# Causal masking of transposed scores on GpSimd instead of TensorE, with the last units and the stores of later query parts reordered

## What is computed

```python
q = q * cos + _rotate_half(q) * sin
k = k * cos + _rotate_half(k) * sin
qg = q.reshape(b, HKV, G, t, DH)                       # HKV 8, G 4, t 1024, DH 16
scores = jnp.einsum('bhgtd,bhkd->bhgtk', qg, k) / math.sqrt(DH)
scores = jnp.where(causal, scores, jnp.finfo(jnp.float32).min)
attn = jax.nn.softmax(scores, axis=-1)
ctx = jnp.einsum('bhgtk,bhkd->bhgtd', attn, v)
```

## Time and profile before

| | |
|---|---|
| median of 3 runs | 854.83 us (853.3 to 856.59) |
| the profiled execution | 854.79 us, span of its instructions 853.0 us |
| mean granted PE clock | 0.944 of full |
| PE busy | 751.9 us (88%) |
| DVE, ACT, POOL busy | 477.2, 314.7, 265.9 us |
| exponentials of the heads | from 91.4 us to 380.4 us |

### The profile page before, as it was taken

How to read it: one execution, slowest core, us unless ns; L and a number is a source line. 1 busy time by engine, 2 the same in 40 slices (tenths; PEclk the granted TensorE clock), 3 DMA queues, 4 the chain that set the end, 5 groups by cost and what they waited for, 6 DMA issues and landing times.

```text
span 853.0 us, 10154 instructions
## 1 busy us (share of the span) xinstructions
PE 751.9 (88%) x3710; PEld 444.2 (52%) x3710; DVE 477.2 (56%) x720; ACT 314.7 (37%) x528; POOL 265.9 (31%) x219
## 2 busy tenths in 40 slices
PE   5797983999999999879889999797778899997998
PEld 2343331333333333217658888543346688885886
DVE  3768761667776767306845637793687433336310
ACT  4211352566665656761315510244212322332100
POOL 0318547431312303151236513232223122222500
PEclk9997896999999999999989999998779899998999
DMA  9360623061321410212003300110320011111111
GB/s 323 129 122 2 146 65 83 1 146 44 68 84 27 110 64 1 91 38 62 0 27 112 97 1 1 52 41 1 48 63 29 25 50 49 49 39 36 61 62 38
DMA packets 24111, 53.00 MB, mean 62 GB/s; under 512 B 4252, under 2 KB 8100, under 8 KB 23044
## 3 DMA queue, kind: packets, MB, share of 16 engines
q1 hardware_dynamic: 24068, 52.44, 22.1%
HBM read 45.63 MB, written 6.60 MB: 61 GB/s over the span
## 4 chain that ended last, share of the span: by engine, by line
PE 67%; DVE 11%; issue 8%; POOL 8%; ACT 3%; DMA 2%; SPq 1%; ACTq 0%; POOLq 0%; DVEq 0%
PE ps L833 65%; DVE mxp L1688 2%; ACT pr L1374 2%; DVE xnb L1565 1%; DMA rq<-in_mask 1%; POOL wsum L2100 1%; PE ps L850 1%; PE ps L982 1%; POOL qacc L2070 1%; POOL qsw L2069 1%; POOL qacc L2073 1%; POOL qparts L2004 1%; DVE st L1543 1%; DVE arena L1572 1%; DVE dg L1912 1%
## 5 line engine op out<-in xcount | busy, mean ns | idle before, releaser
L833 PE MATMUL ps<-arena 128*128 128x512 f32 (+1 forms) x1416 | 333.6, 397 | 13.0 <-ACT full L1499 5.4
L833 PEld LDWEIGHTS ps<-arena 128*128 128x128 f32 (+1 forms) x1416 | 266.0, 189 | 74.7 <-DVE arena L1575 11.8
L1688 DVE TENSOR_REDUCE mxp<-ps 128x2 f32<-128x1024 f32 (+3 forms) x160 | 173.4, 1115 | 85.6 <-PE ps L833 69.2
L1374 ACT ACTIVATE pr<-ps 128x512 f32<-128x512 f32 x288 | 161.6, 596 | 118.8 <-PE ps L833 117.0
L833 PE MATMUL ps<-Qst,Kst 99*128 99x512 bf16 x288 | 106.1, 391 | 7.1 <-ACT pr L1374 4.2
L833 PE MATMUL ps<-Kst,Qst 96*128 96x512 bf16 (+3 forms) x384 | 102.6, 339 | 6.5 <-DVE mxp L1688 4.8
L833 PE MATMUL ps<-pr,vr 128*32 128x512 f32 x576 | 79.4, 624 | 0.7 <-ACT pr L1374 0.7
L833 PE MATMUL ps<-maskb,identb 128*128 128x128 bf16 (+1 forms) x320 | 75.3, 258 | 0.0
L833 PEld LDWEIGHTS ps<-Kst,Qst 96*128 96x128 bf16 x384 | 36.4, 100 | 73.1 <-DVE mxp L1688 27.5
L833 PEld LDWEIGHTS ps<-Qst,Kst 99*128 99x128 bf16 x288 | 27.3, 98 | 77.0 <-ACT pr L1374 58.4
L2191 POOL TENSOR_TENSOR arena<-raw,arena 128x1024 fp32r<-128x1024 f32 x11 | 26.6, 2418 | 85.8 <-ACT arena L1440 85.8
(11 more groups left out here) (190 smaller groups left out, 809.8 us busy)
## 6 DMA issues: line engine op xcount, KB each, us to landing
wmr<-in_wmr SPq DMA_DIRECT2D x8, 1280.0 KB, 6.4
raw<-in_w SPq DMA_DIRECT2D x16, 512.0 KB, 3.3
Qst<-q_parts SPq DMA_DIRECT2D x42, 128.0 KB
q_parts<-qparts SPq DMA_DIRECT2D x3, 768.0 KB, 8.5
x<-in_x SPq DMA_DIRECT2D x8, 256.0 KB, 5.9
wm<-in_wm SPq DMA_DIRECT2D x4, 512.0 KB, 7.1
raw<-in_up SPq DMA_DIRECT2D x8, 256.0 KB, 2.6
raw<-in_down SPq DMA_DIRECT2D x8, 256.0 KB, 2.7
```

What stands on the lines that cost most here:

```text
L833: return nc.tensor.matmul(outp, lhs, rhs, start=start, stop=stop, skip_group_check=True)
L1374: A(pr[:, k % PRING, :], ps[:, 4 + k % 2, :], ACT.Exp, scale=float(DH) ** -0.5).then_inc(exp_done, 1)
L1688: V.tensor_reduce(mxp[:, kh, g0:g0 + heads, i].rearrange("p (b e) -> p b e", e=per), units, AXX, ALU.max)\
```

## The change

It does six things.

- Chunk 1 of the later queries is stored ahead of `head_dmas(0)`, and chunk h+2 after the loads for head h+2 (h = 0, 1), so chunks 2 and 3 are stored ahead of `head_dmas(1)` and `head_dmas(2)`.
- DVE's wait for chunk 3 moves from the start of body 1 to `ctx_norm(0)`.
- For heads 1 to 7 the mask product of `t_unit` is left out. After the exponential GpSimd multiplies the four diagonal blocks, read as int32, by 0 or 1 (`cap`, made once by DVE). PE waits for `masked` before each `pv_round` whose round has a diagonal.
- Diagonal units come early: rounds 0 to 4 hold 1, 2, 2, 2 and 1 of them, rounds 5 to 8 none.
- `pv_round(n, r)` comes after unit 4r+7, for r up to 7, where it was 4r+5.
- "max" comes two units later (unit 26 in a steady body), and `weigh(n+1)` is cut into pieces, one per round from round 1, behind that round's masks.

```diff
@@ body_steps
-        out.append((max(step, 3) if what == "ctx" else step, what, d, s))
+        out.append((max(step, 3) if what == "ctx" else step + 2 * (what == "max"), what, d, s))
@@ transposed_units
-            units.append((r, p) if r <= p else (r - p - 1, NT - 1 - p))
+            if r <= p:
+                units.append((r, p))
+            else:
+                i = NT - 1 - p
+                units.append((i, i) if r == p + 1 else (r - p - 2, i))
...
+DIAG = [[k for k in range(4 * r, 4 * r + 4) if TUNITS[k][0] == TUNITS[k][1]] for r in range(ROUNDS)]
+DIAGS_TO = [sum(len(DIAG[q]) for q in range(r + 1)) for r in range(ROUNDS)]
+POOL_MASKED = 1
+def masks_by_gpsimd(n, r):
+    return NT * (n - POOL_MASKED) + DIAGS_TO[r]
...
+        cap = at("cap", [P, P], I32, HT_B + 28 * 1024)
@@ sync
+            def store_queries(c):
+                sp.wait_ge(part_q, c)
+                sp.dma_start(qscr[c, :, :, :].rearrange("q p t -> p q t"), qparts[:, :, :]).then_inc(q_out, 16)
+            store_queries(1)
             for h in range(NKV):
                 head_dmas(h)
-                if h < 3:
-                    sp.wait_ge(part_q, h + 1)
-                    sp.dma_start(qscr[h + 1, :, :, :].rearrange("q p t -> p q t"), qparts[:, :, :]).then_inc(q_out, 16)
                 if h < NKV - 2:
...
                     load_queries(h + 2, every, st_in[h + 2])
+                if h < 2:
+                    store_queries(h + 2)
@@ tensor, t_unit
-                last = mm(o, Kst[...], Qst[...], True, i > j)
-                if i == j:
+                by_pe = i == j and n < POOL_MASKED
+                last = mm(o, Kst[...], Qst[...], True, not by_pe)
+                if by_pe:
                     last = mm(o, identb[:, :], maskb[:, 1, :].unsqueeze(1).to_broadcast([P, G, P]), False, True)
@@ tensor, pv_round
                 pe.wait_ge(exp_done, n * NTU + 4 * r + 4)
+                if n >= POOL_MASKED and DIAG[r]:
+                    pe.wait_ge(masked, masks_by_gpsimd(n, r))
@@ tensor, head_body
-                    if k % 4 == 1:
-                        if k > 4:
-                            pv_round(n, k // 4 - 1)
-                        elif n:
-                            pv_round(n - 1, ROUNDS - 1)
+                    if k % 4 == 3 and k > 4:
+                        pv_round(n, k // 4 - 1)
+                    if k == 1 and n:
+                        pv_round(n - 1, ROUNDS - 1)
@@ vector
             V.tensor_copy(maskb[:, :, :].rearrange("p a b -> p (a b)"), rq[0][:, 0:2 * P]).then_inc(k_ones, 1)
+            V.tensor_scalar(cap[:, :], rq[0][:, P:2 * P], 0.0, None, ALU.is_ge).then_inc(cap_ready, 1)
...
+            dve.wait_ge(cap_ready, 1)
@@ vector, ctx_norm
+                if n == 0:
+                    dve.wait_ge(part_q, 3)
@@ vector, bodies
-                if n == 1:
-                    dve.wait_ge(part_q, 3)
@@ gpsimd
+            def mask_round(n, r):
+                for k in DIAG[r]:
+                    pool.wait_ge(exp_done, n * NTU + k + 1)
+                    v = pr[:, k % PRING, :].rearrange("p (g t) -> p g t", g=G).bitcast(I32)
+                    nc.gpsimd.tensor_tensor(v, v, cap[:, :].unsqueeze(1).to_broadcast([P, G, P]), ALU.mult).then_inc(masked, 1)
+            def head_pool(n):
+                head_v(n)
+                work = weighing(n + 1) if n < NKV - 1 else iter(())
+                for r in range(ROUNDS):
+                    mask_round(n, r)
+                    if r > 0:
+                        next(work, None)
+                for _ in work:
+                    pass
...
-            head_v(1)
-            weigh(2)
+            pool.wait_ge(cap_ready, 1)
+            head_pool(1)
...
             for n in range(2, NKV):
-                head_v(n)
-                if n < NKV - 1:
-                    weigh(n + 1)
+                head_pool(n)
```

More of the change, by code:

```diff
@@ L21 @@
 F32R = mybir.dt.float32r
+I32 = mybir.dt.int32
 BF16 = mybir.dt.bfloat16
@@ L378 @@
 for i in range(NT):
-    assert [j for j, k in TUNITS if k == i] == list(range(i + 1))
+    assert sorted(j for j, k in TUNITS if k == i) == list(range(i + 1))
+FIRST_J = [next(j for j, k in TUNITS if k == i) for i in range(NT)]
+LAST_J = [[j for j, k in TUNITS if k == i][-1] for i in range(NT)]
+DIAG = [[k for k in range(4 * r, 4 * r + 4) if TUNITS[k][0] == TUNITS[k][1]] for r in range(ROUNDS)]
+DIAGS_TO = [sum(len(DIAG[q]) for q in range(r + 1)) for r in range(ROUNDS)]
+assert DIAGS_TO[-1] == NT
+POOL_MASKED = 1
+def masks_by_gpsimd(n, r):
+    return NT * (n - POOL_MASKED) + DIAGS_TO[r]
 def adaln_two_blocks(nc, a, out):
@@ L560, in adaln_two_blocks @@
         sw_done = sem("later_queries_swapped")
+        cap_ready, masked = sem("cap_ready"), sem("diagonal_masked")
         kst_ones = sem("key_rows_of_ones_ready")
@@ L955, in t_unit @@
                 o = ps[:, 4 + k % 2, :].rearrange("p (g t) -> p g t", g=G)
-                last = mm(o, Kst[:, n % 3, j * P:(j + 1) * P], Qst[:, n % 3, :, i * P:(i + 1) * P], True, i > j)
-                if i == j:
+                by_pe = i == j and n < POOL_MASKED
+                last = mm(o, Kst[:, n % 3, j * P:(j + 1) * P], Qst[:, n % 3, :, i * P:(i + 1) * P], True, not by_pe)
+                if by_pe:
                     last = mm(o, identb[:, :], maskb[:, 1, :].unsqueeze(1).to_broadcast([P, G, P]), False, True)
@@ L971, in pv_round @@
                     q = 32 * strip(i)
-                    last = mm(ps[q:q + 32, 6 + i // 4, :], vr[:, j, :], pr[:, k % PRING, :], j == 0, j == i)
+                    last = mm(ps[q:q + 32, 6 + i // 4, :], vr[:, j, :], pr[:, k % PRING, :], j == FIRST_J[i],
+                              j == LAST_J[i])
                 last.then_inc(pv_done, 1)
@@ L2082, in head_v, with weighing @@
                 nc.gpsimd.tensor_copy(vr[:, :, 0:DH], vtok[:, :, n * DH:(n + 1) * DH]).then_inc(vr_ready, 1)
-            def weigh(h):
+            def weighing(h):
                 pool.wait_ge(wmr_in, 16 * h + 16)
@@ L2102, in weigh @@
                                 link(ins)
+                            yield
                 ins.then_inc(wsum_ready, 1)
+                yield
+            def weigh(h):
+                for _ in weighing(h):
+                    pass
[12 more added lines that the diff above has]
+                for _ in work:
+                    pass
             rope_queries(1)
```

## The result

The changed kernel takes 841.79 us (median of 4 runs, 840.46 to 843.66) where the kernel before takes 855.71 (853.3 to 856.6) beside it: a ratio of 0.9843 [0.9811, 0.9875]. The forecast was 828, the range 815 to 850. The sign and the range hold; the gain is 13.9 us in place of 26.8, about half. In the profiled executions the span falls from 853.0 to 838.6 us, by 14.4.

A forecast was written before the change was run, and what follows sets the result against it. PE was taken as the bound in the heads, with room on DVE, ACT and POOL. The sum: 854.8 - 16.3 - 9.1 - 8.0 + 1.5 + 4.0 + 0.3 + 1.0 = 828.2 us, range 815 to 850.

The forecast's parts named there:

- The stores: Early chunk stores bring chunk 3 forward and remove head 1's whole excess: 16.3 us gained, bounds 13.9 and 16.3.
- The mask products on PE: Mask products leave PE in heads 1 to 7: 9.1 us gained, bounds 5 and 12.3.
- "max" two units later: PE's hole before the turn of the maxima, waiting for nm, is covered: 8.0 us gained, bounds 4 and 11.2.
- mod late next: nothing: After the later "max", DVE's copy of "mod" has 2 us of other PE work ahead, so costs nothing.
- The small costs: DVE making cap in the prologue, 0.3 us, and maxima(1) beside chunk 3, 1.0 us, bounds 0 and 2.
- The split of the output weights: Pushed back by head 7's masks, done by 385 before the projection at 388.59: no cost, 3 us of cover.
- POOL's charges: Two costs of PE waiting for POOL: 1.5 us for masks over all heads, 4.0 us for weigh(3) in head 2.
- weigh(3) late in head 2: Head 3's eight-piece weigh ends late, PE stands before "mod" in head 2: 4.0 us cost, bounds 2 and 6.
- The waits for masks: POOL's 17.3 us before round 4 fit an 18.75 us window; short PE waits cost 1.5 us, bounds 0 and 6.
- The slow integer product: Rival: a GpSimd mask takes 2.56 us, GpSimd becomes the bound, kernel slower at 884.7 us; chance 0.14.
- The partly slow product: Rival: a GpSimd mask takes 1.75 us, adding 14 us of waits, 841 us in all; chance 0.14.
- Chunk 3: Rival: early stores don't bring chunk 3 forward, head 1's hole stays at 14 to 16 us, 844.5 us; chance 0.04.

The follow-up runs named there:

- e1: To the kernel before, only the early stores of the query chunks and DVE's wait moved to ctx_norm(0): 840.73 us, ratio 0.9847.
- e2: The changed kernel with the masks of all heads back on PE as products, GpSimd doing only weigh: 828.75 us, ratio 0.9698.
- e4: The changed kernel with weigh(n+2) done whole behind head n's masks, weigh(2) before head 1, its weights loaded earlier: 821.95 us, ratio 0.9628.
- e8: e1 plus "max" and pv_round both two units later, diagonals where they were, masks on PE: 831.73 us, ratio 0.9694.
- e6: The changed kernel with each GpSimd mask product done twice, the second waiting for the first: 909.34 us (2 runs), ratio 1.062.
- e3: The changed kernel with weighing pausing after its first product too, so the first piece is one product: 833.93 us, ratio 0.9769.

## Why the prediction was right or wrong

**The stores** (16.3): right for head 1, 16.34 by e1; by the medians e1 brings 13.6 (854.37 - 840.73), and head 0 is 2.1 us longer in its profile. The starts of both chunks are within 1.5 us of those forecast, and no wait of DVE for `qparts` is left.

**The mask products on PE** (9.1, of it 1.4 a head): right, 33.05 - 31.67 = 1.38 a head between e2 and e4, which differ in the place of the weighing too. From the start of head 7 to its turn it is 29.17 us in e2 and 28.57 in e4, 0.6 less where 0.7 was taken (half of 8 x 0.22 would have been 0.9). But the gain is there only when POOL keeps up.

**"max" two units later** (8.0, bounds 4 and 11.2): too small, and wrong in cause. By the heads 1 to 6, e1 to e2 gives 204.06 - 196.29 = 7.8. Head 0, for which the sum had little more than 1.3, is 4.1 us shorter besides (59.70 and 55.56 us between the copies), and by the medians it is 12.0 (840.73 - 828.75). The stretch around the turn of the maxima in head 0, first e1, then e2:

```profile
119.00:126.00 7.00, 5.68 (x41) 2.92 (x42) 3.84 (x9) 2.44 (x5) 1.13 (x1) 0.76 0.08 15
```

```profile
118.00:125.00 7.00, 5.42 (x47) 2.60 (x47) 6.06 (x10) 3.71 (x7) 3.23 (x3) 1.00 0.02 4
```

With the wait of 3.0 us for `nm` the slow stretch behind it goes as well; the forecast counted holes alone. It also let "max" and `pv_round` share one cover of 1.3 us a head; the runs give `pv_round` all of it in the steady heads. And "mod late next: nothing" fails: DVE's copy costs 1.6 us with "max" alone, and in the change itself PE stood 2.0 us for it, in heads 0 and 1.

**The small costs.** For the maxima beside chunk 3 the forecast had 1.0; `nm` took 1.99 in place of 1.14 us in e1, 0.85 more. The mask's 0.3 I can't tell apart. The split of the output weights, "nothing", holds: it is done at 364.98 and the projection begins at 371.52. What cost 1.1 us is the split of `fc1` behind it, which the step didn't follow. Later, from the projection to the end, the profile after has 467.1 us against 464.4 before, in unchanged work, with a granted clock of 0.91 and 0.85 in two stretches of 100 us against 0.93 and 0.86. e1 and e4 have 464.9, e8, with no masks on GpSimd, 466.4, and e6 469.3. So the same work differs there by some microseconds between profiles, and whether the change has a part in it stays open.

**The terms outside POOL's charges, together.** They fit e4 to 0.8 us, and part of that is luck, as errors cancel:

| step | by the medians | in the sum |
|---|---|---|
| before to e1: stores, small operations beside chunk 3 | 13.6 | 16.3 - 1.0 = 15.3 |
| e1 to e2: "max", `pv_round`, diagonals, `cap` | 12.0 | 8.0 - 0.3 = 7.7 |
| e2 to e4: mask products | 6.8 | 9.1 |
| together | 32.4 | 32.1 |

The interval of a ratio is 2.4 us to either side in these kernels, so of the three errors only the middle one, 4.3 us, is clear, and the rows of the heads show it too. The upward bounds, listed with 4 for the waits where 6 - 1.5 is 4.5, reach 846 and not 845; that changes nothing in the argument.

**weigh(3) late in head 2** (4.0, bounds 2 to 6): right within its bounds. PE stood 3.1 us for `wsum`, and behind it ran slow. The stretch from 186 to 192 us after:

```profile
186.00:192.00 6.00, 4.12 (x26) 1.52 (x27) 2.17 (x3) 0.60 (x1) 1.65 (x2) 0.55 0.18 33
```

A granted clock of 0.55 is close to 1.2 of 2.4 GHz. PE is busy 33.16 us in that head and 30.55 in head 2 of e4; these 2.6 us and the wait are 5.7 of the 5.78 that head 2 costs. The term took the wait without the slow stretch that its own bound named.

**The waits for masks** (1.5, bounds 0 to 6): here the prediction failed. The step is "the pieces of rounds 1 to 3 (0.9 + 2 x 2.54 = 6.0)". The pieces are 3.4 + 2 x 2.5 = 8.4, since the first holds two products and a sum, so POOL needs 17.3 + 2.4 = 19.7 us for a window of 18.75. The trace of head 4 has the terms: from the copy at 235.95 to the end of round 4's mask at 256.24 it is 20.3 us, 18.5 of them work (two masks take 2.48, less than the 2.76 taken) and 1.8 a wait for the exponentials of round 1, which the forecast's queue didn't have. PE comes to round 4 at 256.56, or 18.1 us behind the copy without its own two waits. Besides, I set the window by round 4 and called rounds 2 and 3 "tighter" without working them out, and it is there that PE waits, 0.72 and 1.82 us in a steady head. The prediction named more than about 1 us a head as a sign of being wrong, and it came. The heads 1 and 3 to 6 are 14.2 us over e4 in place of 1.5. By the same heads e3 takes 6.3 of them away, 2.0 in each of heads 3 to 5: that is the part of the misread piece. The other part, 0.7 us in a steady head, is the tight rounds even with the pieces as I read them (0.55 us of PE's waits ahead of round 3). In head 1 e3 has instead the drawn-out operations of DVE shown there.

The two charges together: 5.5 forecast, 19.8 by the medians, and 13.6 us is what the forecast missed by (841.79 - 828.2 = 13.6, of them 14.3 here).

**The rivals.** The slow integer product is refuted: 1.276 us. The partly slow product forecast 841, and 841.8 came, but by no part of its mechanism: the mask is at its f32 price, and the window was short instead of the mask long. Its arithmetic, 8 us a head for each us a mask, came out at 7.0 in e6. Chunk 3 is not late. The Trainium skill, "GPSIMD Engine Reference", section 3.1, puts `tensor_tensor` at the floor that two inputs set on the read port, and not at loop overhead (with 2.6 cycles per element there, where the forecast wrote some 2.5). It has no row for integer products; the 1.276 us of both types here are in line with it. Its section 4.1 advises against elementwise products on GpSimd; here it is the order that decides: the same masks cost 13.0 us with the weighing between them (after against e2) and bring 6.8 with it behind (e4 against e2).

## What to carry to other kernels

When work is moved to an engine with much free time, what counts is not its share of the span but the time of each deadline: write the engine's queue out between two of them, with every instruction in it, for the tightest round and not for the last. Pieces of work without a near deadline belong behind those with one, as e4 shows, with 19.8 us, nearly all of it for a change of order. For each stretch of such a queue, count the waits for its inputs as well as its work. A generator's `yield` is best counted in instructions, against its indentation. When two edits aim at one hole, run each alone: here one of them did all of it in the steady heads. When a sum comes out right, check its terms by themselves: here one of them was 4.3 us too small, and the others made up for it.

## What the runs showed of the hardware

- An int32 product 128x512 on GpSimd takes 1.276 us, as the f32 one does, for 56 instances.
- Very small operations of DVE are drawn out beside a two-input operation of GpSimd: 128x32 from 0.19 to 1.99 us (e1), 32x128 from 0.28 to 1.66 (e4 and e3), 128x4 from at most 0.37 for two to 1.99 for two, as here by source line in the kernel after:

```profile
L1787 DVE TENSOR_SCALAR modc<-modc x2: 171/979/1787, 366.7 to 368.5; 128x4 f32<-128x4 f32 x2
```

  One of the two takes 0.17 us, the other 1.79; it is done when POOL's operation of 2.37 us is (366.08 + 2.37 = 368.45). A tensor-scalar form that reads one tensor isn't spared.
- A single wait of PE of 3.1 us was followed by six microseconds at a granted clock of 0.55, one of 3.0 (e1, to 120.32) by the five from 120 us at 0.66, one of 2.4 (e3) by six at 0.74; the waits of 1.8 us in each steady head were not followed by any (1.00).
